# Moving two power-of-two scales and two vector steps in the attention part of a fused cross-attention and FFN kernel

## The chip, the core and the metric

The kernel runs on one NeuronCore of a Trainium2 chip. The metric is device time in microseconds (us), the median of several executions. The engines are TensorE (PE in the profile, with its weight loads as PEld), VectorE (DVE), ScalarE (ACT), GpSimd (POOL) and SyncE (SP), which here issues every DMA. Each engine takes its instructions strictly in the order written and waits at semaphores for the others.

## The reference

The input x has 16 batches of 512 rows of 512 numbers, the context 16 batches of 120 rows.

```python
def reference(x, ctx_1024, Wq, Wk, Wv, Wo, w_gate, w_up, w_down):
    # cross attention: 16 heads of 32, rotary embedding on q and k, softmax over 120 keys
    x = x + xattn(layernorm(x), ctx_1024, ctx_1024, Wq, Wk, Wv, Wo)
    # gated FFN: 4-bit block weights, activations rounded to 16 bits after each product
    x = x + ffn(layernorm(x), w_gate, w_up, w_down)
    return x
```

Both layer norms subtract the mean and divide by the root of variance plus 1e-5. The change touches only the attention.

## The kernel before, in words

The attention is a software pipeline of 67 steps `s` (`NSTEP`). A unit is one batch and one group of four heads, so a batch takes four steps, and `b, c = divmod(s, 4)`. I call the step of a batch c0, c1, c2 or c3 by its `c`, and the four steps from a c0 on a round. In each step TensorE does, in this order: the scores of unit s-7 (L664 and L671, into the four banks 0 to 3), the query projection of unit s (L689), the score maxima's products of unit s-2 (L712, into banks 0 to 3 again), one output projection (L748), in c2 a transposition of the maxima (L722), and the products with V and the sums (L767, L772).

Banks 0 to 3 pass from hand to hand. ACT's exponential P (L971) must have read the scores before TensorE may write L712's products there, and DVE's maximum MX (L1337) must have read those before the next scores. Around this chain stand these helpers:

- *Layer norm of x.* Two batches ahead of their use, DVE computes mean and variance (`dve_x_stats`, in c3), GpSimd the power -0.5 (`pool_deviation`), and DVE the shift, minus mean times factor (`dve_x_shift`, L1156, in c0). ACT normalises X in place with four copies (`act_normal`, L929, end of c0). In c1 ACT makes the high fp16 part of it in two halves (`act_x_high`, L942), DVE subtracts for the low part (`dve_x_low`, L1165), and SP issues one transposing DMA that brings both into XD (L433). The factor holds XS = 1024.
- *Rotation of q.* ACT evicts the projection into QE (L994), SP swaps neighbouring partitions by two DMAs into QW (L398, L399), GpSimd multiplies with cosine and sine (L1467, L1476), and DVE adds (L1135).
- *Softmax sums.* In c3 ACT copies the sums (RC), SP writes them out and reads them back as RG (L451, L455). In the c0 that follows DVE takes the reciprocal (`dve_recip`, L1212), for the first two batches also a multiplication with the unit of V (L1215). SP writes RG out (L459) and sends one broadcast RB for each unit (L445), GpSimd multiplies the evicted A with it (L1501, two in c1 and two in c2), ACT makes the high part (L1014) and GpSimd the low part (L1506).
- *Order on SP* in c1: swap of c1, the two broadcasts for c2, the transposing DMA of x. The second broadcast waits for the second L1501 of c1, since it reuses its buffer. In c2 the swap follows.

From unit 8 on, ACT's eviction of A carries the unit of V as its scale (`a_unit`), and RG is left as it is. For batch 0 the high and low parts come from the banks and go into XD directly.

## Time and profile before

| | |
|---|---|
| median of three runs | 2326.45 us (2324.95 to 2327.17) |
| profiled execution, its own time | 2326.45 us |
| its span | 2324.6 us |
| busy, share of the span | PE 95%, DVE 72%, ACT 57%, POOL 30% |
| attention | about the first 795 us |

The profile gives for each engine the time it was busy, and for each group of instructions the idle time of the engine just before them with what ended it. A wait in square brackets stands behind the instruction that waited. A start time counts from the start of the span. MX, P, QE, QW, RB, RG, A and XA are names of tiles: XA holds X and, in its second buffer, the high and low part of x, and `banks` are the accumulators of TensorE.

### The profile page before, as it was taken

Reading aid. Unit: us, or ns where it says so; the run is one execution under the profiler, and the core shown is the slowest. Engines: PE = TensorE matmul, PEld = TensorE weight load, DVE = VectorE, ACT = ScalarE, POOL = GpSimd, SP = SyncE. Lnnn points to the kernel's source line nnn. Section 1 sums busy time; section 2 is a strip of 40 time slices with the busy share of each in tenths; the row PEclk is TensorE's granted clock in tenths of the full one; section 3 lists DMA queues with packets and bytes.
Section 4 is the critical chain, followed back from the end, with each engine's and each line's share of the span. In section 5 each row is a group of like instructions: output and inputs, shape, how many; then the busy total and the mean of one; then the engine's idle time right before and its main releaser. Section 6 shows DMA issues by size and latency. Waiting matters only on the chain. (4 is left out here: it accounts for less than half of the span.)

```text
span 2324.6 us, 31131 instructions
## 1 busy us (share of the span) xinstructions
PE 2203.7 (95%) x12037; PEld 971.1 (42%) x12037; DVE 1685.1 (72%) x1690; ACT 1329.8 (57%) x1299; POOL 701.5 (30%) x655
## 2 busy tenths in 40 slices
PE   5898999999998899999999999999998799999999
PEld 3443333333333444444444444444443344444444
DVE  7656788889876766445543598888888887778773
ACT  3345566666654233222322787877877777777772
POOL 3444566666664301000100264444444000000000
PEclk8899999999999999999999999999999899999999
DMA  6333667777777577888875898877776555655552
GB/s 189 97 103 101 168 173 189 170 193 173 193 169 182 154 232 244 265 245 254 255 229 180 286 336 306 303 283 290 292 281 260 188 223 221 235 220 204 209 217 91
DMA packets 286711, 500.14 MB, mean 215 GB/s; under 512 B 187500, under 2 KB 189804, under 8 KB 249692
## 3 DMA queue, kind: packets, MB, share of 16 engines
q1 hardware_dynamic: 286556, 498.09, 66.9%
q8 instruction: 95, 1.56, 0.3%
q14 instruction: 60, 0.49, 0.1%
HBM read 247.75 MB, written 186.58 MB: 187 GB/s over the span
## 5 line engine op out<-in xcount | busy, mean ns | idle before, releaser
L1694 PE MATMUL banks<-XB,W 128*128 128x512 f16 x2304 | 498.9, 380 | 2.3 <-ACT XB L1720 2.3
L1694 PE MATMUL banks<-XB,WT 128*128 128x512 f16 x2304 | 497.4, 379 | 0.0
L2160 PE MATMUL banks<-W,OH 128*128 128x512 f16 x2256 | 488.8, 380 | 2.5 <-DVE OH L2262 2.5
L1714 ACT ACTIVATE OB<-banks,uns 128x512 f32<-128x512 f32 x384 | 255.7, 684 | 391.2 <-PE banks L1694 388.6
L1694 PEld LDWEIGHTS banks<-XB,W 128*128 128x128 f16 x2304 | 225.7, 98 | 275.1 <-issue 3.4
L1694 PEld LDWEIGHTS banks<-XB,WT 128*128 128x128 f16 x2304 | 225.4, 98 | 271.8
L2160 PEld LDWEIGHTS banks<-W,OH 128*128 128x128 f16 x2256 | 221.1, 98 | 270.2 <-DVE OH L2262 3.0
L1981 POOL TENSOR_TENSOR PR<-GS,OB 128x2048 f32<-128x2048 f32 x46 | 220.6, 4795 | 257.5 <-ACT OB L1714 247.6
L1803 DVE TENSOR_REDUCE amx<-OB 128x1 f32<-128x2048 f32 x48 | 109.7, 2285 | 238.2 <-ACT OB L1714 238.2
L748 PE MATMUL banks<-XC,AH 128*128 128x512 f16 x768 | 179.3, 385 | 3.2 <-POOL AH L1506 1.6
L689 PE MATMUL banks<-XD,WQ 128*128 128x512 f16 x768 | 179.2, 383 | 2.5 <-DVE WQ L1127 1.2
L971 ACT ACTIVATE P<-banks 120x2048 f32<-120x2048 f32 x60 | 112.3, 1871 | 85.0 <-PE banks L671 85.0
L1337 DVE TENSOR_REDUCE MX<-banks 128x16 f32<-128x1920 f32 x64 | 137.6, 2151 | 29.9 <-PE banks L712 29.9
L1945 DVE TENSOR_REDUCE amf<-PR 128x4 f32<-128x2048 f32 x47 | 107.5, 2286 | 52.4 <-POOL PR L1981 52.1
L2223 ACT ACTIVATE OH<-OQ 128x2048 f16<-128x2048 int16 x47 | 89.5, 1904 | 95.3 <-DVE OQ L2257 94.3
L2285 DVE SCALAR_TENSOR_TENSOR Y<-banks,gm,XRd 128x512 f32<-128x512 f32 x64 | 46.4, 747 | 118.1 <-PE banks L2160 117.9
L1476 POOL TENSOR_TENSOR QW<-QW,sq 128x512 f32<-128x512 f32 x64 | 86.4, 1350 | 126.3 <-DMA QW<-QE 126.3
L689 PEld LDWEIGHTS banks<-XD,WQ 128*128 128x128 f16 x768 | 70.6, 98 | 116.8 <-issue 38.0
L2243 DVE SCALAR_TENSOR_TENSOR GSd<-SQd,XD 128x2048 f32<-128x2048 int32 x47 | 107.6, 2290 | 15.2 <-ACT SQd L2205 15.2
L1927 DVE SCALAR_TENSOR_TENSOR GS<-SQ,GQ 128x2048 f32<-128x2048 int32 x48 | 109.5, 2282 | 9.8 <-ACT SQ L1902 9.8
L1135 DVE TENSOR_TENSOR QR<-QR,QW 128x512 f32<-128x512 f32 x64 | 73.1, 1142 | 52.3 <-POOL QW L1476 52.3
L1929 DVE TENSOR_REDUCE amg<-GS 128x1 f32<-128x2048 f32 x48 | 109.7, 2286 | 1.7
(272 smaller groups left out, 2904.5 us busy)
## 6 DMA issues: line engine op xcount, KB each, us to landing
g_s<-OB SPq DMA_DIRECT2D x48, 1024.0 KB, 6.1
GL<-g_s SPq DMA_DIRECT2D x48, 1024.0 KB, 7.5
up_s<-OB SPq DMA_DIRECT2D x48, 1024.0 KB, 4.9
XA<-up_s SPq DMA_DIRECT2D x32, 1024.0 KB, 9.3
gq_s<-GQ SPq DMA_DIRECT2D x48, 512.0 KB, 4.8
XD<-gq_s SPq DMA_DIRECT2D x48, 512.0 KB, 6.7
XA<-in_x SPq DMA_DIRECT2D x16, 1024.0 KB, 6.7
QW<-QE SPq DMA_DIRECT2D x128, 128.0 KB, 2.9
```

Source lines behind the costliest of these rows:

```text
L689: t = e.matmul(BQ_.rearrange("p (j t) -> p j t", j=4), WQ[:, a, k, c * 128:(c + 1) * 128], XT[b % 2][:, xa, :, k, :], start=(n == 0 and k ...
L748: t = e.matmul(o_bank(u), AH[b % 2][:, a, k, j * 128:(j + 1) * 128], WO[:, wa, k, :], start=(n == 0), stop=(n == 11))
L971: e.activation(P[0:SK], PB[0:SK, 0:4, :], ACT.Exp, scale=SM_SCALE).then_inc(s_p, 1)
L1337: e.tensor_reduce(MX[mb % 2][:, :, :, mc].rearrange("p j g -> p g j"), PB[:, 0:4, 0:4 * SK].rearrange("p g (j s) -> p g j s", j=4), AX.X, ...
L1694: t = e.matmul(pk[:].rearrange("p (j t) -> p j t", j=4), WT[w][:, ot, wa, kk, :], XB[i % 2][:, xa, :, kk, :], start=(kk == 0 and wa == 0 a ...
L1714: e.activation(OB[n % 3][:, r, :], bank[(k + 4) % 8][:], ACT.Copy, scale=uns[:, 12 * w + ot:12 * w + ot + 1]).then_inc(s_ev, 1)
L1803: e.tensor_reduce(amx[:, m:m + 1], flat(OB[m % 3][:]), AX.X, ALU.max, apply_absolute_value=True).then_inc(s_gr, 1)
L1927: e.scalar_tensor_tensor(GS[m % 2][:], SQ[m % 2][:], 65535.0, GQ[m % 2][:], ALU.min, ALU.mult).then_inc(s_gs, 1)
L1929: e.tensor_reduce(amg[:, m:m + 1], GS[m % 2][:], AX.X, ALU.max, apply_absolute_value=True).then_inc(s_gsm, 1)
L1981: e.tensor_tensor(PR[:], GS[m % 2][:].rearrange("p (a t) -> p a t", a=4), OB[(NC + m) % 3][:], ALU.mult).then_inc(s_pr, 1)
L2160: t = e.matmul(pk[:].rearrange("p (r n) -> p r n", r=4), OH[i % 2][:, a, ot, j * 128:(j + 1) * 128], WD[:, :, c, wa, o4, :], start=(ot == ...
L2243: e.scalar_tensor_tensor(GSd[:], sqd(m), 65535.0, AL[m % 3], ALU.min, ALU.mult).then_inc(s_dgs, 1)
```

## The change

Four things change.

1. XS leaves the factor of the layer norm and becomes an immediate scale of the two high copies, and the low part multiplies with it in the same instruction (SCALAR_TENSOR_TENSOR for TENSOR_TENSOR).
2. The unit of V leaves the evictions of A. Every RG is now multiplied with it after the reciprocal, and the last batch's four products take it as a second multiplication.
3. For steps from 16 on, ACT makes the high part of x at the start of c1, ahead of P. Before, it stood behind the eviction of QE and the two half copies.
4. For the same steps, DVE makes the low part ahead of MX of c1 and not behind it, and the shift behind MX of c0 and not ahead of it.

```diff
@@ -345,13 +345,6 @@
             xr, x1 = ((QE[0][:], QW[0][:]), (QE[1][:], QW[1][:]), (RX[:, 0, :], RX[:, 2, :]), (RX[:, 1, :], RX[:, 3, :]))[i]
             return xr, x1, i, 16 * (m + 1 + (LATE // 2 if i < 2 else 0))
 
-        def rr(b):
-
-            return 2 * b + 2 if b < 2 else b + 3
-
-        def a_unit(u):
-            return vun[:, 1:2] if u >= 8 else 1.0
-
         bc = lambda a: a.unsqueeze(2).to_broadcast([128, 16, 32])
         v3 = lambda a: a.rearrange("p (b i) -> p b i", i=32)
 
@@ -455,7 +448,7 @@
             e.dma_start(RG[:], sr_d[0].rearrange("r (e f) -> (r e) f", f=64)).then_inc(s_rl, 16)
 
         def dma_recip_out(e, b):
-            e.wait_ge(s_rr, rr(b))
+            e.wait_ge(s_rr, 2 * (b + 1))
             e.dma_start(sr_d[1 + b % 2].rearrange("r (e f) -> (r e) f", f=64), RG[:]).then_inc(s_rd, 16)
 
         def sp_x1_out(e, u):
@@ -933,13 +926,13 @@
             if b == 0:
                 for h in range(2):
                     e.wait_ge(s_tp, 2 + h)
-                    e.activation(XD[0][:, 0, 2 * h:2 * h + 2, :], PB[:, 2 * h:2 * h + 2, :], ACT.Copy).then_inc(s_xhi, 1)
+                    e.activation(XD[0][:, 0, 2 * h:2 * h + 2, :], PB[:, 2 * h:2 * h + 2, :], ACT.Copy, scale=XS).then_inc(s_xhi, 1)
                 return
             e.wait_ge(s_ln, 4 * b + 4)
             if b >= 2:
                 e.wait_ge(s_xt, 16 * (b - 1))
             for h in range(2):
-                e.activation(ST[:, 0, 2 * h:2 * h + 2, :], X[:, 2 * h:2 * h + 2, :], ACT.Copy).then_inc(s_xhi, 1)
+                e.activation(ST[:, 0, 2 * h:2 * h + 2, :], X[:, 2 * h:2 * h + 2, :], ACT.Copy, scale=XS).then_inc(s_xhi, 1)
 
         def act_largest(e, b):
 
@@ -961,6 +954,8 @@
             for s in range(NSTEP):
                 b, c = divmod(s, 4)
                 kv = list(kv_at(s))
+                for nb in x_at(s, 2) if s >= 16 else []:
+                    act_x_high(e, nb)
                 u = s - 7
                 if 0 <= u < NU:
                     e.wait_ge(s_c1, u + 1)
@@ -977,9 +972,7 @@
                         e.wait_ge(s_alo, u - 5)
                     elif u == 0:
                         e.wait_ge(s_clo, 3)
-                    if u == 8:
-                        e.wait_ge(s_vu, 2)
-                    e.activation(A[:, u % 6, :], BP_, ACT.Copy, scale=a_unit(u)).then_inc(s_a, 1)
+                    e.activation(A[:, u % 6, :], BP_, ACT.Copy).then_inc(s_a, 1)
                 if c == 3 and 0 <= b - 2 < B:
                     e.wait_ge(s_sum, 4 * (b - 2) + 4)
                     if b >= 3:
@@ -994,8 +987,6 @@
                     e.activation(QE[n % 2][:], BQ_, ACT.Copy, scale=qsc[:]).then_inc(s_qe, 1)
                 if HALF <= s - 1 < NU:
                     act_half(e, s - 1)
-                for nb in x_at(s, 2) if s >= 16 else []:
-                    act_x_high(e, nb)
                 if s == 1:
                     act_split(e, 2)
                     act_ctx(e, 1)
@@ -1039,7 +1030,7 @@
             e.activation(RC[:], BS_, ACT.Copy).then_inc(s_rc, 1)
             e.wait_ge(s_pv, u + 1)
             e.wait_ge(s_alo, u - 5)
-            e.activation(A[:, u % 6, :], BP_, ACT.Copy, scale=a_unit(u)).then_inc(s_a, 1)
+            e.activation(A[:, u % 6, :], BP_, ACT.Copy).then_inc(s_a, 1)
             for u in range(NU - 4, NU):
                 e.wait_ge(s_c1, u + 1)
                 e.wait_ge(s_sum, u)
@@ -1047,7 +1038,7 @@
                 if u < NU - 1:
                     e.wait_ge(s_pv, u + 1)
                     e.wait_ge(s_q, NU)
-                    e.activation(AZ[:, u - NU + 4, :], BP_, ACT.Copy, scale=a_unit(u)).then_inc(s_a, 1)
+                    e.activation(AZ[:, u - NU + 4, :], BP_, ACT.Copy).then_inc(s_a, 1)
             for u in range(NU - 8, NU - 4):
                 if u < NU - 6:
                     e.wait_ge(s_an, u + 1)
@@ -1059,8 +1050,8 @@
             e.wait_ge(s_rg, 64 * (B - 1))
             e.activation(RC[:], BS_, ACT.Copy).then_inc(s_rc, 1)
             e.wait_ge(s_pv, NU)
-            e.activation(AZ[:, 3, :], BP_, ACT.Copy, scale=a_unit(NU - 1)).then_inc(s_a, 1)
-            e.wait_ge(s_rr, rr(B - 1))
+            e.activation(AZ[:, 3, :], BP_, ACT.Copy).then_inc(s_a, 1)
+            e.wait_ge(s_rr, 2 * B - 1)
             e.wait_ge(s_sum, NU)
             for j in range(4):
                 e.activation(P[:, j, :].rearrange("p (c g r) -> p c g r", c=4, g=4),
@@ -1159,11 +1150,11 @@
             for h in range(2):
                 e.wait_ge(s_xhi, 2 * b + h + 1)
                 if b == 0:
-                    e.tensor_tensor(XD[0][:, 1, 2 * h:2 * h + 2, :], PB[:, 2 * h:2 * h + 2, :], XD[0][:, 0, 2 * h:2 * h + 2, :],
-                                    ALU.subtract).then_inc(s_xlo, 1)
+                    e.scalar_tensor_tensor(XD[0][:, 1, 2 * h:2 * h + 2, :], PB[:, 2 * h:2 * h + 2, :], XS,
+                                           XD[0][:, 0, 2 * h:2 * h + 2, :], ALU.mult, ALU.subtract).then_inc(s_xlo, 1)
                     continue
-                e.tensor_tensor(ST[:, 1, 2 * h:2 * h + 2, :], X[:, 2 * h:2 * h + 2, :], ST[:, 0, 2 * h:2 * h + 2, :],
-                                ALU.subtract).then_inc(s_xlo, 1)
+                e.scalar_tensor_tensor(ST[:, 1, 2 * h:2 * h + 2, :], X[:, 2 * h:2 * h + 2, :], XS, ST[:, 0, 2 * h:2 * h + 2, :],
+                                       ALU.mult, ALU.subtract).then_inc(s_xlo, 1)
 
         def dve_x1_aggregate(e, b):
 
@@ -1210,16 +1201,16 @@
             if b == 0:
                 e.wait_ge(s_vu, 2)
             e.reciprocal(RG[:], RG[:]).then_inc(s_rr, 1)
-            if b < 2:
-                e.wait_ge(s_rr, 2 * b + 1)
-                e.tensor_scalar(RG[:], RG[:], vun[:, 1:2], None, ALU.mult).then_inc(s_rr, 1)
+            e.wait_ge(s_rr, 2 * b + 1)
+            e.tensor_scalar(RG[:], RG[:], vun[:, 1:2], None, ALU.mult).then_inc(s_rr, 1)
 
         def dve_last(e, j):
 
             e.wait_ge(s_rx, j + 1)
             e.wait_ge(s_a, NU)
             part = AZ[:, :, j * 128:(j + 1) * 128]
-            e.tensor_tensor(part, part, bank[6 + j % 2].rearrange("p (c t) -> p c t", c=4), ALU.mult).then_inc(s_dn, 1)
+            e.scalar_tensor_tensor(part, part, vun[:, 1:2], bank[6 + j % 2].rearrange("p (c t) -> p c t", c=4),
+                                   ALU.mult, ALU.mult).then_inc(s_dn, 1)
 
         def dve_normal_unit(e, u):
 
@@ -1320,9 +1311,8 @@
                 if c == 0 and 0 <= b - 3 < B:
                     dve_recip(e, b - 3)
 
-
-                for nb in x_at(s, 1) if s >= 16 else []:
-                    dve_x_shift(e, nb)
+                for nb in x_at(s, 2) if s >= 16 else []:
+                    dve_x_low(e, nb)
                 if s in (11, 12):
                     dve_amax(e, {11: 7, 12: 8}[s])
 
@@ -1369,9 +1359,9 @@
                 for ob in deviations_at(s):
                     dve_x1_aggregate(e, ob)
 
-                for nb in x_at(s, 1) if s < 16 else []:
+                for nb in x_at(s, 1):
                     dve_x_shift(e, nb)
-                for nb in [1] if s == 2 else x_at(s, 2):
+                for nb in [1] if s == 2 else x_at(s, 2) if s < 16 else []:
                     dve_x_low(e, nb)
                 for nb in x_at(s, 0):
                     dve_x_stats(e, nb)
@@ -1481,7 +1471,7 @@
             e.wait_ge(s_lmv, b + 1)
             if b >= 2:
                 e.wait_ge(s_ln, 4 * (b - 2) + 4)
-            e.tensor_scalar(q[:, 0:4], mv1[b % 2][:, :, 1], 1e-5, 1.0 / (XS * XS), ALU.add, ALU.mult).then_inc(s_lrs, 1)
+            e.tensor_scalar(q[:, 0:4], mv1[b % 2][:, :, 1], 1e-5, 1.0, ALU.add, ALU.mult).then_inc(s_lrs, 1)
             e.wait_ge(s_lrs, 2 * b + 1)
             e.tensor_tensor(q[:, 0:4], q[:, 0:4], mh[:], ALU.pow).then_inc(s_lrs, 1)
 
```

The first two pieces of order are DVE's in one round. Around the reciprocal in c0, before:

```order
L1135 TENSOR_TENSOR QR<-QR,QW 128x512
L1212 RECIPROCAL RG<-RG 128x64
L1156 SCALAR_TENSOR_TENSOR rs<-mv,rs 128x4
L1337 TENSOR_REDUCE MX<-banks 128x4x4
L1258 TENSOR_TENSOR RW<-RW 128x512
```

and now:

```order
L1126 TENSOR_TENSOR QR<-QR,QW 128x512
L1203 RECIPROCAL RG<-RG 128x64
L1205 TENSOR_SCALAR RG<-RG,vun 128x64
L1327 TENSOR_REDUCE MX<-banks 128x4x4
L1147 SCALAR_TENSOR_TENSOR rs<-mv,rs 128x4
L1249 TENSOR_TENSOR RW<-RW 128x512
```

The multiply of RG is new, and the shift `rs` went from ahead of MX to behind it. The step after it, c1, before:

```order
L1205 TENSOR_REDUCE xmn<-RX 128x1
L1135 TENSOR_TENSOR QR<-QR,QW 128x512
L1337 TENSOR_REDUCE MX<-banks 128x4x4
L1172 BN_AGGR mv<-st 128x2 x4
L1165 TENSOR_TENSOR XA<-XA 128x1024 x2
L1187 SCALAR_TENSOR_TENSOR RX<-banks,vun,RX 128x512
```

and now:

```order
L1196 TENSOR_REDUCE xmn<-RX 128x1
L1126 TENSOR_TENSOR QR<-QR,QW 128x512
L1156 SCALAR_TENSOR_TENSOR XA<-XA 128x1024 x2
L1327 TENSOR_REDUCE MX<-banks 128x4x4
L1163 BN_AGGR mv<-st 128x2 x4
L1178 SCALAR_TENSOR_TENSOR RX<-banks,vun,RX 128x512
```

The two halves of the low part went from behind MX to ahead of it. On ACT, from the end of c0 to c2, before:

```order
L910 ACTIVATE QE<-QR 128x512
L929 ACTIVATE XA<-XA,rs 128x512 x4
L971 ACTIVATE P<-banks 120x2048
L982 ACTIVATE A<-banks,vun 128x512
L994 ACTIVATE QE<-banks,qsc 128x512
L909 ACTIVATE W<-W 128x120
L910 ACTIVATE QE<-QR 128x512
L942 ACTIVATE XA<-XA 128x1024 x2
L1014 ACTIVATE AH<-A 128x512 x2
L1034 ACTIVATE RW<-RW 128x512
L971 ACTIVATE P<-banks 120x2048
```

and now:

```order
L903 ACTIVATE QE<-QR 128x512
L922 ACTIVATE XA<-XA,rs 128x512 x4
L935 ACTIVATE XA<-XA 128x1024 x2
L966 ACTIVATE P<-banks 120x2048
L975 ACTIVATE A<-banks 128x512
L987 ACTIVATE QE<-banks,qsc 128x512
L902 ACTIVATE W<-W 128x120
L903 ACTIVATE QE<-QR 128x512
L1005 ACTIVATE AH<-A 128x512 x2
L1025 ACTIVATE RW<-RW 128x512
L966 ACTIVATE P<-banks 120x2048
```

The two halves of the high part follow the four normalising copies directly, with P behind them.

## Rows read from the trace of the kernel before

**Rows 1.** Timeline of DVE, the reciprocals: start us, us, engine, line, op, tiles.

```profile
403.50 0.55 DVE L1212 RECIPROCAL RG<-RG 128x64 f32<-128x64 f32 x1
...
632.60 0.55 DVE L1212 RECIPROCAL RG<-RG 128x64 f32<-128x64 f32 x1
...
668.56 0.55 DVE L1212 RECIPROCAL RG<-RG 128x64 f32<-128x64 f32 x1
```

**Rows 2.** Windows, the eleven rounds: busy us (xcount) of each engine, granted clock, DMA.

```profile
246.00:669.00 423.00, 400.43 (x3046) 150.85 (x3045) 373.46 (x528) 265.60 (x364) 276.34 (x228) 0.99 0.71 180
```

**Rows 3.** Waits of PE from 246 to 669: us in total, times, longest us.

```profile
PE banks L664 <- DVE MX L1337: 13.3, 16, 2.0
PE banks L712 <- ACT P L971: 8.6, 14, 1.2
```

**Rows 4.** Timeline of DVE in the round at 403.50.

```profile
403.96 0.77 DVE L1156 SCALAR_TENSOR_TENSOR rs<-mv,rs 128x4 f32<-128x4 f32 x1
404.66 2.15 DVE L1337 TENSOR_REDUCE MX<-banks 128x16 f32<-128x1920 f32 x1
...
435.18 2.15 DVE L1337 TENSOR_REDUCE MX<-banks 128x16 f32<-128x1920 f32 x1
```

**Rows 5.** Timeline of POOL, c2 of that round.

```profile
432.33 1.26 POOL L1476 TENSOR_TENSOR QW<-QW,sq 128x512 f32<-128x512 f32 x1 [3.38 <-DMA QW<-QE]
```

**Rows 6.** Timeline of PE in that round and the step after it.

```profile
410.84 0.39 PE L712 MATMUL banks<-W,QE 32*128 32x120 f16 x16
...
420.83 0.39 PE L712 MATMUL banks<-W,QE 32*128 32x120 f16 x16 [1.07 <-ACT P L971]
...
430.40 0.39 PE L712 MATMUL banks<-W,QE 32*128 32x120 f16 x16 [0.23 <-ACT P L971]
...
437.38 1.33 PE L664 MATMUL banks<-QR,W 32*120 32x512 f32 x8 [2.04 <-DVE MX L1337]
```

**Rows 7.** Timeline of SP's queue in that round.

```profile
418.34 7.13 SPq L433 DMA_TRANSPOSE XD<-XA  x1
...
427.75 0.53 SPq L398 DMA_DIRECT2D QW<-QE  x1
```

**Rows 8.** ACT's forms of line 982: ns min/median/max, first and last start us.

```profile
L982 ACT ACTIVATE A<-banks,vun x51: 674/682/688, 246.9 to 732.5; 128x512 f32<-128x512 f32 x51
L982 ACT ACTIVATE A<-banks x8: 578/591/598, 153.4 to 237.2; 128x512 f32<-128x512 f32 x8
```

**Rows 9.** DVE's groups by form up to 800: busy us, mean ns, idle before.

```profile
L1165 DVE TENSOR_TENSOR XA<-XA 128x1024 f16<-128x1024 f32 x30 | 45.3, 1550 | 11.9 <-ACT XA L942 11.8
...
L1127 DVE SCALAR_TENSOR_TENSOR XC<-A,wsc,XC 128x2048 f16<-128x2048 f32 x1 | 2.3, 2344 | 0.0
```

**Rows 10.** The same view: DVE's multiply of RG.

```profile
L1215 DVE TENSOR_SCALAR RG<-RG,vun 128x64 f32<-128x64 f32 x2 | 0.5, 254 | 0.1
```

**Rows 11.** Timeline of ACT, c0 and c1 of the round at 403.50.

```profile
404.77 2.93 ACT L929 ACTIVATE XA<-XA,rs 128x512 f32<-128x512 f32 x4 [0.33 <-DVE rs L1156]
408.25 1.88 ACT L971 ACTIVATE P<-banks 120x2048 f32<-120x2048 f32 x1 [0.55 <-PE banks L671]
...
412.66 1.99 ACT L942 ACTIVATE XA<-XA 128x1024 f16<-128x1024 f32 x2
```

**Rows 12.** Timeline of DVE, MX of c0 in another round.

```profile
289.11 2.14 DVE L1337 TENSOR_REDUCE MX<-banks 128x16 f32<-128x1920 f32 x1
```

**Rows 13.** Timeline of PE, the maxima's products of c1 in that round.

```profile
295.28 0.39 PE L712 MATMUL banks<-W,QE 32*128 32x120 f16 x16
```

**Rows 14.** Timeline of POOL, the two multiplies of c1 in that round.

```profile
296.52 1.27 POOL L1501 TENSOR_TENSOR A<-A,RB 128x512 f32<-128x512 f32 x1 [2.81 <-DMA RB<-sr_s]
299.56 2.11 POOL L1501 TENSOR_TENSOR A<-A,RB 128x512 f32<-128x512 f32 x1 [1.76 <-DMA RB<-sr_s]
```

**Rows 15.** Waits of SP's queue from 246 to 669: us in total, times, longest us.

```profile
SPq L398 <- ACT QE L994: 45.2, 23, 4.7
...
SPq L433 <- DVE XA L1165: 8.8, 6, 2.6
```

## Prediction

> **What bounds the kernel now.** I read the table of stretches first, then the waits of the stretch that the edits touch, and last one round of it on each engine. A round is four steps (c0 to c3), and it starts where DVE takes the reciprocal of the softmax sums.
>
> The moved instructions stand in the eleven rounds that end with the reciprocal at 668.56 [rows 1], a stretch of 423.00 us, so 38.4 us a round. In it TensorE works 400.43 us [rows 2], 36.4 a round, so what it waits is time lost. It waits 13.3 us for DVE's maxima MX and 8.6 us for ScalarE's exponentials P [rows 3]. So each round holds about 2 us of slack for TensorE. What makes the round longer than TensorE's work? Follow the round at 403.50. The reciprocal ends, SP writes it out (L459), and two broadcasts RB come back. GpSimd's second multiply (L1501, which waits for its RB) frees a buffer, and SP can send the last broadcast and then the transposing DMA, which holds its queue for 7.13 us. Only then does SP send the rotation's swap (L398 at 427.75). GpSimd waits 3.38 us for it, DVE waits for GpSimd, MX stands at 435.18, and TensorE waits 2.04 us for it. DVE's row work then leads to the next reciprocal, about 8 us behind MX [rows 4 to 7]. I call this chain the ring. TensorE stands beside it and does not set its length in most rounds.
>
> **The change part by part.**
>
> *Scales.* XS moves out of the deviation's factor into the two copies of x, and the unit of V out of the evictions of A into one multiply. The copies keep their number and shape. An immediate scale stands in no pair of rows that differ in it alone. Below it is free; above, a pointer scale costs 0.09 us a copy (682 against 591 ns for A) [rows 8]. I take zero, since those copies are of fixed length and have no pointer. The low part becomes SCALAR_TENSOR_TENSOR: its quiet row is 2344 ns for 2048 columns, so 1.2 us for 1024, and the TENSOR_TENSOR that it replaces has a mean of 1550, overlaps with GpSimd included [rows 9]. I take zero apart from the overlaps below. The bounds are minus 0.35 us apiece (all overlap gone) and plus 0.8 (the mean stretched to its 2344). ACT's 56 copies of A lose that pointer, 0.09 us apiece, and behind each stands a QE that waits for TensorE, so I count nothing. The bounds are minus 5 us and zero. The four last products get a second multiplication and stay one pass: zero.
>
> *One more multiply on RG.* From the third batch on, each reciprocal is followed by a TENSOR_SCALAR. The trace has it twice, 0.25 us long [rows 10], and with the handing over 0.29: the instruction behind a lone reciprocal starts 0.46 us after it, at 403.96 [rows 1, 4], and will start 0.75 after it. This lies on the ring. The bounds are 0.25 and 0.4 us. Ten times in the eleven rounds it makes 2.9 us. Three times behind them it makes 0.9 us.
>
> *The shift behind MX, the high part ahead of P.* In eleven rounds ACT's four normalising copies wait for the shift, and the shift now follows MX. Old order at 404: shift done at 404.73, copies at 404.77 for 2.93 us, P at 408.25, and the high copies (1.99 us) late, at 412.66 [rows 4, 11]. New order: MX starts at 403.50 + 0.75 = 404.25 and ends at 406.4. It starts 0.4 us earlier than before, since the shift no longer waits for GpSimd's power ahead of it. Then shift and handing over 0.2, copies 2.9, high copies 2.0, P 1.9 (as L971 has there): P ends 7.0 us behind MX, at 413.4. TensorE stood ready for its next score maxima at 410.84 [rows 6]. That is a new wait of 2.55 us in step c1. Worst is the round with MX at 289.11: MX end 291.25 + 0.29 + 7.0 = 298.55 against 295.28, 3.3 us [rows 12, 13]. In the first round it is under 1 us, since TensorE itself was late there. Over all eleven, worked out in this way from the same instructions, it makes 25 us.
>
> What lies behind the waiting P? ACT's A and QE, SP's swap of QE, and the score maxima with their MX. In the round at 403.50 the swap of c1 would go out at 414.65 instead of 412.1. GpSimd takes it up only behind its second multiply (about 419), so it is hidden. MX of c2 moves from 421.67 to 422.7, and the ring's swap at 427.75 does not ask for it. By c3 TensorE is 2.55 - 1.07 - 0.23 = 1.25 us late, because the waits of c2 and c3 are swallowed, and the 2.04 us ahead of c0 swallow the rest [rows 6]. The ring's MX of c3 starts 4.4 us behind the end of L712's maxima here, in the tightest round a little over 1 us, and the lateness that reaches it is 2 us or less. So the 25 us fall nearly all into slack. A floor stays: from one MX of c0 to the next a round takes at least 36.7 us (7.0 + 27.5 for TensorE's work from there + 0.05 + 2.15). The shortest round, from 632.60, had 36.0 [rows 1]: plus 0.7 us there, and as much again, my choice, where a short round can't take the ring's gains.
>
> *The low part ahead of MX.* x_low used to stand behind MX of c1, on top of GpSimd's second multiply. That one took 2.11 us at 299.56 and 1.27 where it was alone [rows 14]. Now it ends about 6.4 us behind MX of c0, while DVE would wait for TensorE anyway (until 7.4). Over ten rounds the excess of that multiply over 1.27 sums to 3.0 us, and it lies on the ring: minus 3.0. SP's transpose was held by x_low in six rounds, for 8.8 us in all, 2.6 at the longest [rows 15]. Three of them gain 0.4 (minus 1.2). In the other three, 2.3 to 2.6 us come free, of which QE of c2 and TensorE's floor leave me about 1 each (minus 3, bounds 0 and minus 7.5). For new overlaps with the first multiply of c1 I book plus 1.
>
> The Trainium skill (SBUF — State Buffer, section "Who interferes with whom") has a rule on this: a VectorE instruction with two SBUF inputs and a GpSimd one that reads SBUF exclude each other for the whole instruction. The trace agrees (2.11 against 1.27 us). By that rule the new place can also hurt, as in the round of rows 12, where the first multiply starts at 296.52 within x_low: one of the two would wait about 1.2 us, x_low ending near 299 instead of 298, still about when TensorE delivers. So the sum would be the same to a few tenths.
>
> **Sum.** The ring gives +2.9 - 3.0 - 1.2 - 3.0 = -4.3, floor +1.4, overlaps +1.0, multiplies behind the stretch +0.9: -1.0 us. The profiled execution has a span of 2324.6 and a time of 2326.45, which is also the median, so 2325.5 us.
>
> **Rivals.** What this kernel's timing can tell from no change is about 0.2%, 4.7 us, so faster is below 2321.8 and slower above 2331.1.
> - *The new wait of P stays on TensorE.* Price: each round's new wait less the waits that the same round already had. From the rows of each round this leaves 0 to 1.9 us, 8.7 in sum, and 0.9 behind: 2336. It decides when the swap of c2 or the sums' way out (SP sends them behind QE of c3) follows ACT and not the transpose. For it speaks that SP waits 45 us for QE of ACT in this stretch [rows 15]. Against it: the reciprocal did not wait for its data in these rounds. If nothing at all is absorbed it is 2326.45 + 25 = 2351. Chance 0.28.
> - *The ring shortens fully.* All three held transposes gain their 2.5 us and the floor does not bite: +2.9 + 0.9 - 3.0 - 1.2 - 7.5 = -7.9, 2318.5. For it: in these rounds DVE does wait for GpSimd's QW. Against: the rounds at 37 us have no room. Chance 0.2.
> - *The change does not do what it says*: the copies find ACT idle in both places and nothing but the multiply counts, 3.8 us, 2330. Against: P stood less than 7.0 us behind MX in all eleven rounds. Chance 0.07.
> - My forecast, with its own range 2321.8 to 2331.1: 0.45.
>
> Range for 8 in 10: 2318 to 2339. Faster 0.22 (the second rival and a little of the forecast's edge), same 0.5 (forecast and the third), slower 0.28.
>
> **What would show it.** ACT's high copies start right behind the normalising ones, and P of c1 ends 7 us behind MX of c0. TensorE's waits at L712's instruction for P grow from 8.6 to between 20 and 30 us, while its waits for MX shrink from 13.3 to a few. GpSimd's second multiply takes 1.27 us, and the transpose no longer waits for x_low. The reciprocals stand 38.0 us apart on average. Wrong I am if the distance grows above 38.8, or if the swap of c2 waits for QE instead of the transpose.

## The result, and the profile after

| | before | after |
|---|---|---|
| median in the same series, five runs each | 2327.17 us (2324.95 to 2332.11) | 2343.86 us (2342.65 to 2348.62) |
| ratio | | 1.0073, interval 1.0057 to 1.0089 |
| profiled execution, time and span | 2326.45 and 2324.6 us | 2340.16 and 2338.3 us |

The change makes the kernel 0.7% slower. I had forecast 2325.5 us in a range up to 2339, so the forecast is wrong, and the time lies outside the range. What follows is read from the profiled executions.

Where do the 13.7 us of span lie? Windows with the columns of [rows 2] (the first two numbers are the stretch and its length). First what lies behind the eleven rounds in before, then after, cut at the places that answer:

```profile
669.00:797.00 128.00, 110.16 (x735) 44.74 (x733) 88.90 (x156) 48.19 (x65) 52.84 (x96) 0.95 0.65 157
797.00:2324.60 1527.60, 1499.27 (x6915) 677.99 (x6915) 1070.92 (x838) 915.71 (x753) 265.58 (x239) 0.99 0.70 244
```

```profile
246.00:680.00 434.00, 405.69 (x3018) 152.00 (x3018) 363.62 (x535) 260.88 (x362) 266.88 (x227) 0.97 0.73 174
680.00:810.00 130.00, 110.88 (x735) 45.27 (x732) 89.25 (x157) 46.53 (x63) 51.09 (x57) 0.93 0.66 157
810.00:2338.30 1528.30, 1497.70 (x6915) 677.68 (x6915) 1071.76 (x840) 916.39 (x754) 266.66 (x278) 0.99 0.70 244
```

The eleven rounds that took 423 us [rows 2] take 434, and TensorE is busy for 405.69 us in place of 400.43. The last rounds of the attention take 130 us, 2 more than before, and the FFN takes 0.7 us more. The reciprocals stand 39.5 us apart on average (244.82 to 679.63), where they stood 38.4 apart. I had forecast 38.0 and named 38.8 as the bound beyond which I would be wrong. The other sign that I had named, a swap of c2 that waits for QE, did not come.

What does TensorE wait for in these rounds?

```profile
PE banks L705 <- ACT P L966: 27.8, 11, 3.0
PE banks L657 <- DVE MX L1327: 0.5, 2, 0.3
```

This part came as predicted: the new wait of P is 27.8 us (I had 25), and the waits for MX, 13.3 us in [rows 3], are gone. All waits together rise by only 6.4 us, from 21.9 to 28.3. One round shows how. First DVE, start and duration in us:

```profile
404.92 0.55 DVE L1203 RECIPROCAL RG<-RG 128x64 f32<-128x64 f32 x1
405.50 0.68 DVE L1205 TENSOR_SCALAR RG<-RG,vun 128x64 f32<-128x64 f32 x1
406.10 2.15 DVE L1327 TENSOR_REDUCE MX<-banks 128x16 f32<-128x1920 f32 x1
...
412.73 3.42 DVE L1156 SCALAR_TENSOR_TENSOR XA<-XA 128x1024 f16<-128x1024 f32 x2
...
436.11 2.15 DVE L1327 TENSOR_REDUCE MX<-banks 128x16 f32<-128x1920 f32 x1
```

Then ACT in c0 and c1, which answers to [rows 11]:

```profile
408.35 2.93 ACT L922 ACTIVATE XA<-XA,rs 128x512 f32<-128x512 f32 x4 [2.49 <-DVE rs L1147]
411.31 2.00 ACT L935 ACTIVATE XA<-XA 128x1024 f16<-128x1024 f32 x2
413.22 1.86 ACT L966 ACTIVATE P<-banks 120x2048 f32<-120x2048 f32 x1
...
415.85 0.69 ACT L987 ACTIVATE QE<-banks,qsc 128x512 f32<-128x512 f32 x1 [0.29 <-PE banks L705]
```

TensorE, from its wait in c1 to the next scores:

```profile
415.33 0.39 PE L705 MATMUL banks<-W,QE 32*128 32x120 f16 x16 [2.94 <-ACT P L966]
...
447.49 0.70 PE L657 MATMUL banks<-QR,W 32*120 32x512 f32 x4 [0.23 <-DVE MX L1327]
```

And SP's queue, which answers to [rows 7]:

```profile
416.57 0.52 SPq L391 DMA_DIRECT2D QW<-QE  x1
417.13 0.60 SPq L392 DMA_DIRECT2D QW<-QE  x1
417.83 1.22 SPq L438 DMA_DIRECT2D RB<-sr_s  x2
419.14 8.38 SPq L426 DMA_TRANSPOSE XD<-XA  x1
...
429.81 0.53 SPq L391 DMA_DIRECT2D QW<-QE  x1
```

P of c1 ends at 415.08, 6.8 us behind MX of c0, as forecast. The next thing is not in the forecast. QE of c1 follows P, so the swap of c1 leaves at 416.57. Both broadcasts of c2 are queued behind that swap. By now GpSimd's first multiply is long done and the second ends (at 418.27), so both go out one behind the other, right ahead of the transposing DMA. That DMA then holds the queue for 8.38 us, where it held it for 7.13 us [rows 7]. The swap of c2 follows at 429.81, which is 24.9 us behind the reciprocal. It was 24.3 us in the round of before.

The same view over all eleven rounds, first of before and then of after (min, median and max in ns, first and last start):

```profile
L433 SPq DMA_TRANSPOSE XD<-XA x11: 5192/6729/7878, 264.4 to 648.6; - x11
```

```profile
L426 SPq DMA_TRANSPOSE XD<-XA x11: 8011/8432/8860, 259.2 to 656.3; - x11
```

The longest hold of before is shorter than the shortest of after. SP's waits in these rounds show that its queue now waits longer for ACT. First of before:

```profile
SPq L398 <- ACT QE L994: 45.2, 23, 4.7
...
SPq L443 <- POOL A L1501: 23.9, 12, 3.3
```

and of after:

```profile
SPq L391 <- ACT QE L987: 84.2, 23, 5.4
...
SPq L436 <- POOL A L1491: 0.6, 1, 0.6
```

In before, the two broadcasts left as the multiplies freed their buffers, mostly apart from each other. In after, the queue waits here for QE, and the broadcasts' own wait is over by then, but for one of 0.6 us. The wait of the transpose for x_low [rows 15] is gone.

The following table carries the rest of the study. I worked it out from the timelines of DVE and SP: means over the eleven rounds, in us behind the reciprocal that starts the round. "Swap c1" is when SP sends the swap of c1, "turn" is the transposing DMA, and "next" is the next reciprocal, so the length of the round. The other kernels are the experiments below.

| kernel | swap c1 | turn starts | held | turn ends | swap c2 | MX of c3 | next | ratio |
|---|---|---|---|---|---|---|---|---|
| before | 9.1 | 14.9 | 6.8 | 21.6 | 23.2 | 30.1 | 38.4 | 1 |
| after | 11.8 | 14.5 | 8.4 | 22.9 | 24.5 | 31.5 | 39.5 | 1.0073 |
| e1_moves | 11.2 | 14.0 | 8.6 | 22.6 | 24.1 | 31.1 | 39.1 | 1.0041 |
| e2_scales | 8.7 | 14.6 | 7.1 | 21.7 | 23.2 | 30.2 | 38.7 | 1.0006 |
| e3_fill | 11.9 | 14.6 | 8.5 | 23.1 | 24.5 | 31.7 | 39.8 | 1.0049 |
| e4_shift_ahead | 9.9 | 14.1 | 7.5 | 21.6 | 23.1 | 30.3 | 38.4 | 0.9986 |
| e5_broadcast_first | 11.9 | 14.3 | 7.4 | 21.8 | 23.2 | 30.6 | 38.5 | 0.9998 |
| e6_shift_only | 9.9 | 15.1 | 6.6 | 21.7 | 23.3 | 30.1 | 38.6 | 0.9999 |
| e7_high_low | 9.8 | 14.0 | 7.6 | 21.7 | 23.1 | 30.2 | 38.3 | 0.9981 |
| e8_fold | 9.6 | 13.8 | 7.6 | 21.3 | 22.8 | 29.9 | 37.9 | 0.9980 |
| e9_pair_in_before | 9.3 | 15.7 | 7.6 | 23.3 | 25.0 | 31.7 | 39.9 | 1.0080 |
| e10_multiply_behind | 11.2 | 15.1 | 7.7 | 22.8 | 24.3 | 31.2 | 39.3 | 1.0070 |
| e11_fold_broadcast_first | 10.8 | 13.6 | 7.5 | 21.1 | 22.6 | 30.1 | 38.3 | 0.9981 |
| e12_high_only | 9.6 | 15.0 | 6.5 | 21.5 | 22.9 | 29.9 | 38.5 | 1.0015 |

In all fourteen kernels the swap of c2 leaves 1.4 to 1.7 us behind the end of the transposing DMA, and the next reciprocal comes 16.5 to 17.2 us behind that end. Where it ends by 21.8 us the ratio is 1.0015 or less; where it ends at 22.6 or later it is 1.0041 or more.

### The profile page after: what moved, and what is told of

Same layout as the page of the kernel before. It is cut to its first block and busy times, and to the rows that moved or that the text cites. A ratio compares the mean times of both kernels' runs of the same rounds, so it can differ in the third digit from the quotient of the medians.

```text
span 2338.3 us, 31144 instructions
## 1 busy us (share of the span) xinstructions
PE 2209.0 (94%) x12037; PEld 973.0 (42%) x12037; DVE 1675.0 (72%) x1703; ACT 1325.5 (57%) x1299; POOL 695.5 (30%) x655
## 5 line engine op out<-in xcount | busy, mean ns | idle before, releaser
L741 PE MATMUL banks<-XC,AH 128*128 128x512 f16 x768 | 190.5, 402 | 4.2 <-POOL AH L1496 3.6
L741 PEld LDWEIGHTS banks<-XC,AH 128*128 128x128 f16 x768 | 74.0, 102 | 99.2 <-issue 25.6
```

What stands on the lines that cost most here:

```text
L741: t = e.matmul(o_bank(u), AH[b % 2][:, a, k, j * 128:(j + 1) * 128], WO[:, wa, k, :], start=(n == 0), stop=(n == 11))
```

## The experiments

Ratios are against the kernel before on the same chip. Each time is the median of 6 to 12 executions. Where an expectation names two ranges and the time falls outside both, I say so.

### Which part costs: the moved steps or the scales

**e1_moves** is the kernel before with the moved steps only. **e2_scales** is the kernel after with the steps in their old order.

```diff
 # e1_moves, from before (ACT; DVE likewise: low part ahead of MX, shift behind it)
+                for nb in x_at(s, 2) if s >= 16 else []:
+                    act_x_high(e, nb)
                 u = s - 7
...
                     act_half(e, s - 1)
-                for nb in x_at(s, 2) if s >= 16 else []:
-                    act_x_high(e, nb)
```

> The kernel before with the moved steps alone (high part ahead of P, low part ahead of MX, shift behind MX); scales and reciprocals stay as they were. Theory A, the new wait of TensorE for P in c1 (2.85 us a round, 27.8 us in all), the clock drops behind it and SP's swap behind QE carry the loss: about 2339 us, at least 10 of the 16.7 us, waits for P of c1 still above 20 us. Theory B, the multiply of RG in each round is the main cost: within 5 us of 2327.

Measured: 2338.64 us, ratio 1.0041 (1.0027 to 1.0055), as by theory A. TensorE's waits in the rounds:

```profile
PE banks L712 <- ACT P L973: 21.3, 11, 3.1
PE banks L664 <- DVE MX L1337: 6.0, 6, 2.6
```

> The changed kernel with the old order of the steps: XS and the unit of V as changed, a multiply of RG behind every reciprocal. Theory A: the multiply is 0.25 to 1.2 us on the ring (it lies on top of a GpSimd multiply) but the ring has no other change, so +3 to +8 us: 2330 to 2335. Theory B: 2338 or more.

Measured: 2329.61 us, ratio 1.0006 (0.9996 to 1.0016), just below theory A's range. The scales, the multiply of RG included, cost nothing that can be told while the steps stand where they stood. The moves alone cost 0.4%, and together with the scales 0.7%. So the larger part lies in the moves, and the scales add to it only on top of them.

### Which of the moves

**e4_shift_ahead** is after with the shift back ahead of MX, **e6_shift_only** is after with the high and the low part back in their old places, **e7_high_low** is before with only those two moved, and **e12_high_only** is before with only the high part moved.

```diff
 # e4_shift_ahead, from after (DVE)
+                for nb in x_at(s, 1) if s >= 16 else []:
+                    dve_x_shift(e, nb)
                 for nb in x_at(s, 2) if s >= 16 else []:
                     dve_x_low(e, nb)
...
-                for nb in x_at(s, 1):
+                for nb in x_at(s, 1) if s < 16 else []:
                     dve_x_shift(e, nb)
 # e6_shift_only, from after: act_x_high again behind act_half, dve_x_low again behind the shift
 # e7_high_low, from before (DVE; on ACT as in e1_moves)
                     dve_x_shift(e, nb)
+                for nb in x_at(s, 2) if s >= 16 else []:
+                    dve_x_low(e, nb)
 # e12_high_only, from before: the ACT part of e1_moves alone
```

> The changed kernel with the shift back ahead of MX in c0, all else as changed. ACT's four copies then start about 2.1 us earlier, so P of c1 ends 4.7 us behind MX instead of 6.9 and TensorE waits about 0.7 us instead of 2.85, with no halved clock. Theory A: 2328 to 2334. Theory B (multiply of RG): 2340 or more. If the low part ahead of MX is what costs: also 2340 or more.

Measured: 2327.97 us, 0.9986 (0.9977 to 0.9995), at the lower edge of theory A's range. Its swap of c1 leaves at 9.9 us in place of 11.8, and TensorE's waits are close to those of before again:

```profile
PE banks L657 <- DVE MX L1329: 14.0, 17, 2.1
PE banks L705 <- ACT P L966: 8.1, 11, 0.9
```

> The changed kernel with high and low part back at their old places, so that only the shift is moved (and the multiply of RG stays). Normalising copies then end 3.1 us behind MX of c0 and P 5.0 us behind it, TensorE waits about 0.9 us in c1 and QE is 2 us earlier than in the changed kernel. If the shift behind MX costs by way of P alone: 2331 to 2336. If it costs in any order: 2341 or more.

Measured: 2328.79 us, 0.9999 (0.9987 to 1.0011). This is less than either range that I had named: alone, the late shift costs nothing that can be told.

> The kernel before with high part ahead of P and low part ahead of MX, the shift at its old place ahead of MX, no further multiply. If these two moves are what gained in the run with the shift ahead (ratio 0.9986) and the multiply cost it something: 2320 to 2325. If the gain came from the scales: 2327 or more.

Measured: 2326.69 us, 0.9981 (0.9969 to 0.9992). The time lies between my two ranges; against the kernel before in its own series (2329.82 us) it is a gain of 0.2%.

> The kernel before with only ACT's high part moved ahead of P (low part and shift at their old places). If the gain of the run with high and low part moved (ratio 0.998) comes from the low part leaving GpSimd's second multiply alone: 2326 to 2330 here. If it comes from ACT having the high part out of the way of QE and the high parts of A: 2321 to 2325.

Measured: 2330.39 us, 1.0015 (1.0005 to 1.0025), just above the first range.

So neither the late shift nor the early high part costs much by itself. Against before (9.1) each leaves the swap of c1 only 0.6 to 0.8 us later. Both together make it 2.1 us later with the old scales and 2.7 with the new ones, and only then does the queue behind it suffer. The low part ahead of MX is what separates e7 from e12: 0.9981 against 1.0015. It lets the transposing DMA start 1 us earlier, but that one is then held 1.2 us longer, so the way of this gain isn't to be read from the table.

### Is it SP's queue?

**e5_broadcast_first** is after with one edit on SP: the first broadcast of c2 is sent ahead of the swap of c1 and not behind it. ACT, DVE and TensorE keep their order, so P is as late as in after.

```diff
+                first = normal_at(s + 1)[:1] if c == 1 and s >= 16 else []
+                for u in first:
+                    dma_recip(e, u)
                 if s < NU:
                     sp_swap(e, ROT["q", s], 512)
...
-                for u in normal_at(s + 1):
+                for u in normal_at(s + 1)[len(first):]:
                     dma_recip(e, u)
```

> The changed kernel; in c1 of the steps from 16 on SP sends the first broadcast of c2 ahead of the swap of c1. If the transposing DMA holds SP's queue for 8.4 us (6.7 before the change) because both broadcasts now leave in one piece right ahead of it, it falls towards 7, and as it stands on the ring the time falls by up to 11 us: 2333 to 2339. If the hold lies beside what sets the round: 2342 to 2345.

Measured: 2328.74 us, ratio 0.9998 (0.9986 to 1.0011), below both ranges: the edit gives back more than I expected. TensorE's only wait in the rounds:

```profile
PE banks L708 <- ACT P L969: 24.1, 17, 2.9
```

and SP's queue in one round, with the view of the transposing DMA over all rounds below it:

```profile
411.28 0.52 SPq L438 DMA_DIRECT2D RB<-sr_s  x1
411.90 0.53 SPq L391 DMA_DIRECT2D QW<-QE  x1
412.48 0.59 SPq L392 DMA_DIRECT2D QW<-QE  x1
413.87 0.57 SPq L438 DMA_DIRECT2D RB<-sr_s  x1
414.54 7.28 SPq L426 DMA_TRANSPOSE XD<-XA  x1
```

```profile
L426 SPq DMA_TRANSPOSE XD<-XA x11: 6554/7400/8192, 260.1 to 645.8; - x11
```

The whole loss is gone while TensorE still waits 24.1 us for P. So the wait of P, which I had priced as the danger, does not set the time. The order and the timing in SP's queue do, unless it is the clock, which the next section looks at. The swap of c1 leaves as late as in after (11.9 us), the hold falls from a median of 8.43 to 7.40 us, and the round from 39.5 to 38.5.

Could the earlier broadcast help simply by landing earlier? In after GpSimd waits for a broadcast of c2 in one round of the eleven only (1.15 us), so its landing was not what held the round. What GpSimd waits for there is the swap of c2: in all eleven rounds of after, 43.4 us in sum. In e5 it does so in four rounds, 2.1 us in sum. In the others it comes to the swap of c2 late by itself, because it now waits for the swap of c1, behind the broadcast: 34.0 us in sum, where it waited 2.7 in after. A still earlier end of the transposing DMA would thus bring little in e5.

**e9_pair_in_before** is the counterpart: the kernel before, with no step moved and no scale changed. The first broadcast of c2 is made to wait for the same multiply as the second, so that both leave together, late.

```diff
             elif u >= 2:
-                e.wait_ge(s_an, u - 1)
+                e.wait_ge(s_an, u if c == 2 and u >= 6 else u - 1)
```

> The kernel before with one wait more: the first broadcast of c2 also waits for GpSimd's second multiply of c1, so that both broadcasts leave in one piece right ahead of the transposing DMA. Nothing is moved on ACT or DVE. If it is this pairing that makes the DMA hold SP's queue longer, the hold rises from 6.7 (median) towards 8.4 us and the time by 5 to 15 us: 2333 to 2343. If the longer hold of the changed kernel had another cause (the earlier low part), hold and time stay within 0.3 us and 5 us.

Measured: 2343.53 us, ratio 1.0080 (1.0066 to 1.0094), about the same loss as the change's, and just above the range. Two rounds, and the DMA over all rounds:

```profile
374.26 0.52 SPq L398 DMA_DIRECT2D QW<-QE  x1
...
379.49 1.23 SPq L445 DMA_DIRECT2D RB<-sr_s  x2
380.81 9.10 SPq L433 DMA_TRANSPOSE XD<-XA  x1
...
417.22 0.52 SPq L398 DMA_DIRECT2D QW<-QE  x1
417.79 0.60 SPq L399 DMA_DIRECT2D QW<-QE  x1
419.77 1.23 SPq L445 DMA_DIRECT2D RB<-sr_s  x2
423.02 6.41 SPq L433 DMA_TRANSPOSE XD<-XA  x1
```

```profile
L433 SPq DMA_TRANSPOSE XD<-XA x11: 5977/7011/9095, 264.0 to 664.3; - x11
```

Here TensorE waits for MX (23.5 us), and for P no longer than before (8.7 us). The hold grows less than in after (mean 7.6 us; the median, 7.0, hardly grows), and the DMA starts 0.8 us later; both add to a swap of c2 at 25.0. So the loss needs no late P. It needs the broadcasts to leave late and the transposing DMA to end late, whatever causes that.

The eleven rounds are of two kinds, and they tell what the hold goes with. In five, as in the first one shown, the DMA follows the pair of broadcasts at once (1.3 us behind the first), and it is held for 8.4 to 9.1 us. In the other six, as in the second, it starts 3.2 us or more behind the first broadcast, and is held for 6.0 to 7.0. The swap of c1 had left long before in both kinds. So it is the broadcasts right ahead of the DMA that go with the long hold. The swap of c1 seems to matter only because it holds them back: in e5 it leaves 2.5 us ahead of the DMA, as late as in after, and the hold is 7.4 us. The other kernels agree. Where the first broadcast leaves 1.4 us ahead of the DMA on average (after, e1) the mean hold is 8.4 and 8.6 us. At 2.6 ahead (e7, e8) it is 7.6, at 3.6 (e5) 7.4, and at 4.1 (before) 6.8.

### TensorE's clock

Behind the waits for P the trace of after has a second effect. The round at 323.52:

```profile
334.44 0.39 PE L705 MATMUL banks<-W,QE 32*128 32x120 f16 x16 [2.85 <-ACT P L966]
334.76 4.45 PE L741 MATMUL banks<-XC,AH 128*128 128x512 f16 x12
```

The same twelve products take 2.76 us where the clock stays up. The windows of this stretch have the granted clock in the third column from the right:

```profile
335.50:338.50 3.00, 3.00 (x9) 1.08 (x8) 2.11 (x5) 2.52 (x6) 2.62 (x3) 0.50 0.36 132
339.50:342.50 3.00, 3.00 (x29) 0.82 (x22) 2.97 (x5) 0.11 (x1) 2.92 (x4) 1.00 1.83 125
```

That is the lower level, 1.2 GHz, and then the upper again. Read in steps of half a microsecond, the low stretch lasts 3.4 us. Nine rounds of after have a wait of 2.85 to 2.99 us for P, and behind seven of these the clock falls; in the rounds of before it falls once in this way (behind the wait of 2.04 us at 437.38 in [rows 6]). At 1.69 us each the six more are 10 us of TensorE's work at the most. Its busy time shows 5.3 more, with 28 matmul records fewer in the trace. Is that part of the loss? The question is serious, since the low clock goes with the loss: in the rounds it lasts about 24 us in sum in after, 20 in e9, 17 in e1 and in e10, and 7 or less in each of the others. e5 took queue and clock back together, so it can't tell them apart. **e3_fill** is after with ten query products computed twice in c1 of every round, in the place where TensorE would wait (operands shortened here).

```diff
+                if n == 0 and u >= 16 and c == 1:
+                    for r in range(10):
+                        e.matmul(BQ_..., WQ[:, a, r % 4, ...], XT[...], start=(r == 0), stop=(r == 9))
```

> The changed kernel; in c1 of the steps from 16 on, TensorE first computes ten of the products of the query projection once more (2.3 us) and overwrites them, so that it is at work while P is still missing. The output is the same. If the halved clock after the wait (7 of 11 rounds, 1.7 us each) counts in the time: the clock stays full, waits for P of c1 fall to about 0.6 us, time 2332 to 2338. If the ring through SP and DVE sets the round and TensorE's lost clock lies beside it: 2343 to 2345.

Measured: 2341.69 us, 1.0049 (1.0037 to 1.0061), between my two ranges. Its rounds in the windows, and TensorE's waits in them:

```profile
246.00:683.00 437.00, 420.70 (x3151) 161.02 (x3150) 373.41 (x537) 262.08 (x363) 272.69 (x228) 1.00 0.74 173
```

```profile
PE banks L709 <- ACT P L970: 8.2, 10, 0.9
PE banks L657 <- DVE MX L1331: 8.0, 15, 1.5
```

The clock stays at 1.00, and the rounds are no shorter: 437.4 us between the outer reciprocals, against 434.8. The waits for MX come back. So the halved clock does not set the round; what it took from TensorE lay beside SP's queue, like the waits. One reserve: the added products are work themselves, so the run can't show what a full clock alone would give. The two ratios differ by 0.24%, but their intervals touch, and in the profile the difference lies behind the eleven rounds. The mean granted clock of the whole execution is 0.986 in e3, 0.977 in after and 0.980 in before. Whether the clock costs something outside the rounds, up to this 0.24%, stays open.

### The place of the multiply

**e10_multiply_behind** is after with the multiply of RG behind MX of c0 in batches 2 to 13. MX of c0 comes 0.7 us earlier on average, and SP sends RG 1.3 us later.

```diff
             e.reciprocal(RG[:], RG[:]).then_inc(s_rr, 1)
+            if not 2 <= b <= 13:
+                dve_unit(e, b)
...
+                if c == 0 and 2 <= b - 3 <= 13:
+                    dve_unit(e, b - 3)
```

> The changed kernel with the multiply of RG behind MX of c0 and not ahead of it. MX, and with it P of c1, comes 0.3 to 1.2 us earlier; RG leaves about 2.3 us later. If the way from MX through P, QE and SP's swap sets the round: 2334 to 2340, waits for P near 2.2 us. If the way from RG through the broadcasts and the second multiply of c1 sets it: 2345 to 2365.

Measured: 2343.04 us, 1.0070 (1.0058 to 1.0082), as after, and between my two ranges. The swap of c1 is 0.6 us earlier and the DMA is held for less (7.7 us), but it starts 0.6 us later, which I put down to the later RG and its broadcasts. The ends differ by 0.2 us. The multiply itself, of after and then of e10:

```profile
L1205 DVE TENSOR_SCALAR RG<-RG,vun x11: 254/685/1356, 245.4 to 642.0; 128x64 f32<-128x64 f32 x11
```

```profile
L1209 DVE TENSOR_SCALAR RG<-RG,vun x11: 232/240/256, 246.0 to 642.3; 128x64 f32<-128x64 f32 x11
```

### Versions that gain

**e8_fold** is e4 with the unit of V as the scale of the copy RC (one pointer scale a batch), so that neither the evictions of A nor RG need it. **e11_fold_broadcast_first** is e8 with the edit of e5.

```diff
-                    e.activation(RC[:], BS_, ACT.Copy).then_inc(s_rc, 1)
+                    e.activation(RC[:], BS_, ACT.Copy, scale=vun[:, 0:1] if b >= 4 else 1.0).then_inc(s_rc, 1)
...
-            e.wait_ge(s_rr, 2 * b + 1)
-            e.tensor_scalar(RG[:], RG[:], vun[:, 1:2], None, ALU.mult).then_inc(s_rr, 1)
+            if b < 2:
+                e.wait_ge(s_rr, 2 * b + 1)
+                e.tensor_scalar(RG[:], RG[:], vun[:, 1:2], None, ALU.mult).then_inc(s_rr, 1)
```

> The changed kernel with the shift ahead of MX and the unit of V as the scale of ACT's copy of the sums from the fifth batch on, so that neither RG nor A nor the last products are multiplied with it. The multiply of RG (median 0.68 us, 11 or more on the ring) falls away for 0.09 us on ACT: 2318 to 2324. If the multiply is hidden there: 2326 to 2328.

Measured: 2325.19 us, 0.9980 (0.9969 to 0.9990), between my two ranges. Against e4 (0.9986) the multiply of RG is worth nothing that can be told.

> The version with the shift ahead and the unit of V folded into the copy of the sums (ratio 0.998), with the first broadcast of c2 ahead of the swap of c1 as well. If the hold of the transposing DMA is still on the ring there: 2315 to 2322. If TensorE's own work and waits for P set the round by now: 2322 to 2327.

Measured: 2323.57 us, 0.9981 (0.9969 to 0.9993). Both beat before and after. The gain over before is 0.2%, just what this kernel's timing can tell. On top of e8 the broadcast's new place brings nothing. In e8 GpSimd waits 30.2 us for the swap of c2 in the eleven rounds, in e11 only 2.0. But there it waits 34.1 us for the swap of c1, which leaves 1.2 us later and behind a broadcast, and in e8 only 1.2.

## Why the prediction was wrong, point by point

- *The new wait of P.* Right in mechanism and size. P ends 6.8 us behind MX (7.0 forecast), the waits sum to 27.8 us (25 forecast, 20 to 30 named), the longest is 3.0.
- *It falls nearly all into slack.* Right for the waits themselves, as e5 shows: there 24.1 us of them cost nothing. It is also why this number was a poor guide. TensorE's waits and its work add up to the round whatever sets its length, and in after they only fill a round that SP's queue had made longer.
- *"GpSimd takes it up only behind its second multiply (about 419), so it is hidden."* This is the step that failed, and with it the term that the ring was given for the transposing DMA, 7.13 us of hold in both kernels. I followed the swap of c1 to the engine that uses it, and there it is indeed hidden. I did not follow it in its queue. Behind it stand both broadcasts of c2, the transposing DMA and the swap of c2. I had written that the queue's order is just this, and that the DMA holds the queue for 7.13 us, and took those 7.13 us as fixed. They are not. The late swap holds the first broadcast back until it stands 1.4 us ahead of the DMA instead of 4.1, and the mean hold goes from 6.8 to 8.4 us. That this order on SP makes the loss is shown by e5 (loss gone) and e9 (loss made without any move).
- *The sizes.* My ring had -4.3 us in eleven rounds, 0.4 a round. The DMA does start 0.4 us a round earlier. The longer hold adds 1.7, so its end and the swap of c2 come 1.3 us later. The next reciprocal comes 1.1 us a round later: 12.6 us over the eleven rounds. The first of them starts 1.5 us earlier, and all that lies behind them takes 2.6 us more; together the 13.7 of the span.
- *The multiply of RG.* Booked at 0.25 us, measured at 0.69 in the median and up to 1.36. It runs at 405.50 beside GpSimd's L1457, which starts at 404.76. The Trainium skill (SBUF — State Buffer, "Who interferes with whom") lists tensor_scalar among the VectorE operations that can take the port pair shared with GpSimd. The trace agrees: 0.24 us where nothing of GpSimd's runs beside it (e10). I had used that page for two-input operations only. So MX of c0 did not come 0.4 us earlier, as I had it, but 0.1 later on average (1.3 us behind the reciprocal, 1.2 in before). By e2 the multiply costs nothing alone. On top of the moves it is what e1 lacks, together with the scales: 1.0041 against 1.0073, with intervals that barely part. It delays two things, the late P with the swap of c1 (0.6 us against e1) and RG's way out (0.8 us). Which of them carries the difference is not shown: e10 eases the first at the cost of the second and gains nothing.
- *The scales, the low part.* e2 stands at 1.0006, so the scales are right. The low part ahead of MX brings a gain, as e7 against e12 shows, but not by an earlier end of the transpose. GpSimd's second multiply takes 1.3 us in every round, as forecast (up to 2.11 before, [rows 14]). But the low part now lies on its first multiply, which takes 1.5 to 1.95 us in ten rounds where it took 1.27: 5.1 us in sum, where I had booked 1.0 for new overlaps. Most of that is hidden, since the second multiply waits for its own broadcast behind it (1.92 us in the round shown) and starts at the same distance from the reciprocal as before, 12.0 against 11.8 us.
- *The rivals.* "The new wait of P stays on TensorE" named the right region, slower and 2336. It asked whether SP's swap follows ACT and not the transpose. It does, but it is the swap of c1 and not that of c2. The swap of c2 still follows the transpose, 1.3 us later than it did. The price (8.7 us) came from TensorE's waits, and so it had the wrong source as well.

What stays open: why the transposing DMA is held longer when broadcasts of the same queue stand right ahead of it. The Trainium skill (Perfetto Trace Analysis, 'What "DMA-bound" means') says that such a slice on the issuing engine's track is the making of descriptors and not the movement of data. By that, the data's own landing need not move with it. In after the landing also grew, from a median of 9.9 to 10.9 us, and no run here shows what SP does within the hold. That the hold goes with the broadcasts' distance is read from the rounds, e9's above all; I did not run a kernel that changes the hold and nothing else.

## What to carry to other kernels

When a step is delayed on one engine, follow what it releases in two directions: to the engine that uses it, and down the in-order queue in which it stands. A transfer whose own use is well hidden can still hold back everything queued behind it. And a wait of the busiest engine is no price: an edit that leaves the wait and takes the queue's delay away (e5) tells in one run which of the two counts.

## What the runs showed of the hardware

- The transposing DMA held SP's queue for 4.8 us at the least, where the pipeline had just begun, and for 5.2 to 9.4 us in the rounds. Within one kernel (e9) it was 8.4 to 9.1 us with two broadcasts of 256 KB sent in the 1.3 us ahead of it, and 6.0 to 7.0 us with these 3.2 us or more ahead.
- A TENSOR_SCALAR of 128x64 numbers took 0.24 us alone and up to 1.36 us beside a GpSimd multiply.
- TensorE's granted clock fell to 1.2 GHz behind seven of nine single waits of 2.85 to 2.99 us, for 3.4 us each time. The twelve products behind such a wait took 4.2 to 4.45 us in place of 2.76.
